# Orders of the small steps, a 17-pass down product and a written-out loop in a Mamba and FP4-FFN block

## The reference

```python
xz = x @ W_in                                    # 256 -> 2 x 512
x_conv = silu(conv1d(x_proj, 4 taps) + conv_b)   # causal, per channel
ssm = x_conv @ W_xproj                           # 33 columns: delta, B (16), C (16)
delta = softplus(ssm[..., 0])
h_mean = einsum('bld,bln->bdn', x_conv, delta * B) / L
y = (einsum('bdn,bln->bld', h_mean, C) + D * x_conv) * silu(z)
x = layernorm(x + y @ W_out)
h = silu(fp4(x) @ fp4(w_gate).T) * (fp4(x) @ fp4(w_up).T)     # 256 -> 704
out = layernorm(x + fp4(h) @ fp4(w_down).T)                   # 704 -> 256
```

## Time and profile before

| | us |
|---|---|
| median of 3 runs | 2334.24 (2331.59 to 2337.22) |
| the profiled execution | 2339.92 |
| its span, first to last instruction | 2338.1 |

### The profile page before, as it was taken

How to read it: one execution, slowest core, us unless ns; L and a number is a source line. 1 busy time by engine, 2 the same in 40 slices (tenths; PEclk the granted TensorE clock), 3 DMA queues, 4 the chain that set the end, 5 groups by cost and what they waited for, 6 DMA issues and landing times.

```text
span 2338.1 us, 38729 instructions
## 1 busy us (share of the span) xinstructions
PE 2050.8 (88%) x10532; PEld 1615.6 (69%) x10532; DVE 1701.5 (73%) x3292; ACT 1279.5 (55%) x2612; POOL 988.0 (42%) x1643
## 2 busy tenths in 40 slices
PE   2887799999899998999999999899989999888886
PEld 1555577777777777777777777777767777666665
DVE  6223477877787777777777787878778877777775
ACT  2556555655555656555655565555555655433343
POOL 2222344444444444444444444444444444434342
PEclk9879999999999999999999999999999999888898
DMA  2223322222222222222222222222222222111100
GB/s 74 86 72 113 111 93 95 84 86 83 94 85 83 92 96 86 78 88 95 84 92 85 95 84 86 82 87 92 93 83 83 97 84 86 52 57 55 57 30 14
DMA packets 132401, 191.35 MB, mean 82 GB/s; under 512 B 15024, under 2 KB 66096, under 8 KB 132144
## 3 DMA queue, kind: packets, MB, share of 16 engines
q1 hardware_dynamic: 132144, 188.42, 24.4%
HBM read 104.48 MB, written 83.89 MB: 81 GB/s over the span
## 4 chain that ended last, share of the span: by engine, by line
DVE 35%; PE 35%; issue 17%; ACT 10%; DVEq 1%; POOL 1%; SPq 0%; ACTq 0%; DMA 0%; POOLq 0%
PE pgu L483 9%; PE pd L483 7%; PE pc L557 5%; DVE acc L866 5%; DVE hbuf L802 4%; PE pb L483 4%; DVE g L946 4%; DVE hbuf L929 4%; PE pa L483 3%; ACT hbuf L717 2%; DVE hbuf L808 2%; DVE qsx L795 2%; PE pc L569 2%; DVE qsh L795 2%; DVE hqT L938 2%
## 5 line engine op out<-in xcount | busy, mean ns | idle before, releaser
L483 PE MATMUL pgu<-wgu_hi,xqT 128*128 128x512 f32 (+1 forms) x1536 | 437.8, 394 | 3.5 <-ACT xqT L762 1.7
L483 PE MATMUL pd<-wd_hi,hqT 128*128 128x256 f32 (+1 forms) x1536 | 344.9, 306 | 32.6 <-DVE r L959 28.2
L675 ACT ACTIVATE dev<-r,sum 128x256 f32<-128x256 f32 x256 | 130.1, 508 | 405.4 <-DVE r L959 253.9
L427 POOL TENSOR_TENSOR hq<-hnq,qsh 128x704 f32<-128x704 bf16 x128 | 177.7, 1388 | 378.9 <-DVE hnq L811 378.9
L483 PEld LDWEIGHTS pgu<-wgu_hi,xqT 128*128 128x128 f32 x1536 | 286.7, 194 | 68.5 <-issue 6.0
L483 PEld LDWEIGHTS pd<-wd_hi,hqT 128*128 128x128 f32 (+1 forms) x1536 | 267.3, 198 | 59.0 <-issue 38.8
L546 PE MATMUL pd<-wout,g 128*128 128x256 f32 x1024 | 254.8, 392 | 0.0
L483 PE MATMUL pgu<-wgu_lo,xqT 128*128 128x512 f32 (+1 forms) x768 | 233.8, 386 | 0.0
L483 PE MATMUL pd<-wd_lo,hqT 128*128 128x256 f32 (+1 forms) x768 | 224.7, 293 | 0.0
L414 POOL TENSOR_TENSOR acc<-acc,tap 128x512 f32<-128x512 f32 x128 | 163.0, 1274 | 133.9 <-ACT tap L740 133.9
L866 DVE SCALAR_TENSOR_TENSOR acc<-xps,cw,acc 128x512 f32<-128x512 f32 x256 | 195.0, 762 | 33.2 <-POOL acc L414 28.7
(11 more groups left out here) (132 smaller groups left out, 4545.0 us busy)
## 6 DMA issues: line engine op xcount, KB each, us to landing
sz_hbm<-szs SPq DMA_DIRECT2D x128, 256.0 KB, 2.1
xc_hbm<-xcs SPq DMA_DIRECT2D x128, 256.0 KB, 2.0
xl<-xc_hbm SPq DMA_DIRECT2D x128, 256.0 KB, 2.8
zl<-sz_hbm SPq DMA_DIRECT2D x128, 256.0 KB, 3.0
xin<-in_L_attn_x_dram SPq DMA_DIRECT2D x32, 512.0 KB, 4.4
xres<-in_L_attn_x_dram SPq DMA_DIRECT2D x128, 128.0 KB, 2.3
out_dram<-outb SPq DMA_DIRECT2D x128, 128.0 KB, 1.7
scratch<-in_L_attn_W_in_dram SPq DMA_DIRECT2D x1, 1024.0 KB, 7.2
```

The lines of the kernel that those rows point to most:

```text
L427: pool.tensor_tensor(blocks(hq[:, 0:FF]), blocks(hnq[:, :]), spread(qsh[:, 1, :]), ALU.mult).then_inc(hprod_done, 1)
L483: mm = pe.matmul(bank, lhsT, rhs, start=(m == 0), stop=(m == len(pairs) - 1))
L675: act.activation(dev[:, :], r, ACT.Square, bias=total[:, :], scale=-1.0 * DM, accum_out=ssq[:, :]).then_inc(ssq_done, 1)
```

## The change

- VectorE makes the skip product right after gate times up, ahead of h's absolute maximum and low parts. GpSimd multiplies g by silu(z) ahead of adding the first tap.
- ScalarE makes the gate's silu ahead of the conv's, and copies the transposed conv output and transposed x ahead of the squared deviations and the Abs of h.
- The three rows of scales become the innermost axis: an operand steps over three elements.
- `walk` has no loop; all 39 groups are written out.
- The down product's sixth chunk: h's last 64 columns are written twice (GpSimd, one more product), so that their transposes fill 128 rows; the weights hold the high part in rows 0 to 63 and the low part in rows 64 to 127. One pass of 128 rows makes high x high and high x low. At the start GpSimd copies the last 64 weight columns twice, and a zero fill is gone.

```diff
-        qsx = sb("qsx", [P, 3, QX])
+        qsx = sb("qsx", [P, QX, 3])
...
-        qsh = sb("qsh", [P, 3, QH])
+        qsh = sb("qsh", [P, QH, 3])
...
-        def walk(body, fori, last=0):
-
-            for g in range(2 * SPS):
-                body(g, g % SPS, g // SPS)
-            with fori(2, B - last) as b:
-                for s in range(SPS):
-                    body(b * SPS + s, s, b)
-            for g in range(NSUP - last * SPS, NSUP + LAG + 2):
+        def walk(body):
+
+            for g in range(NSUP + LAG + 2):
                 body(g, g % SPS, g // SPS)
...
+            pool.wait_ge(wq_ready, 3)
+            for h in range(KM):
+                rest = quant_w[2][:, h * FF + FC * P:(h + 1) * FF]
+                pool.tensor_copy(twice_d[:, h * P:h * P + FR], rest)
+                last = pool.tensor_copy(twice_d[:, h * P + FR:(h + 1) * P], rest)
+            last.then_inc(wq_ready, 1)
...
                         pool.tensor_copy(hist[:, j, :], xps[:, ST:ST + KC - 1])
-                        wait_apart(pool, (first_tap, u + 1))
-                        pool.tensor_tensor(acc[:, :], acc[:, :], tap0[:, :], ALU.add).then_inc(tap_done, 1)
                     if p2:
 
                         pool.wait_ge(yd_done, w + 1)
                         pool.wait_ge(zl_landed[j % 2], 16 * (2 * i + j // 2 + 1))
                         pool.tensor_tensor(g[:, second(s) % 2, j, :], g[:, second(s) % 2, j, :], zl[:, j % 2, :],
                                            ALU.mult).then_inc(g_ready, 1)
+                    if p1:
+                        wait_apart(pool, (first_tap, u + 1))
+                        pool.tensor_tensor(acc[:, :], acc[:, :], tap0[:, :], ALU.add).then_inc(tap_done, 1)
...
+                        pool.tensor_tensor(blocks(hq[:, FF:(FC + 1) * P]), blocks(hnq[:, FC * P:FF]),
+                                           spread(qsh[:, FC * P // QB:QH, 1]), ALU.mult)
                         pool.tensor_tensor(blocks(hq[:, 0:FF]), blocks(hnq[:, :]),
-                                           spread(qsh[:, 1, :]), ALU.mult).then_inc(hprod_done, 1)
+                                           spread(qsh[:, :, 1]), ALU.mult).then_inc(hprod_done, 1)
...
+                pairs += [(hqT[:, FC, :], wd_hi[:, FC, :]),
+                          (hqT[0:FR, 2 * FC + 1, :], wd_hi[0:FR, FC, :])]
                 split_product(pd[:, 0:DM], DM, pairs).then_inc(dn_pe, 1)
...
+                    if exists(tg):
+                        act.wait_ge(gu_pe, tg + 1)
+                        at_least(act, hq_link, 6 * tg)
+                        act.activation(hbuf[:, 0:FF], pgu[:, 0:FF], ACT.Silu).then_inc(sg_ready, 1)
                     if exists(v):
...
+                    if j != 1 and exists(v):
+                        act.wait_ge(xct_pe, v + 1)
+                        act.activation(xct[:, :, jb * P:(jb + 1) * P],
+                                       pa[:, :].rearrange("p (t n) -> p t n", t=TPS), ACT.Copy)\
+                            .then_inc(xct_copied, 1)
+                    if exists(tx):
+
+                        act.wait_ge(xq_pe, tx + 1)
+                        act.activation(xqT[:, 0:KM, :], pe_[:, 0:DM].rearrange("p (c n) -> p c n", c=KM), ACT.Copy)\
+                            .then_inc(xqT_hi, 1)
                     if exists(to):
                         deviations(r_done, to, r1[:, j, :], sum1, ssq1, ssq1_done)
...
                         dve.tensor_tensor(h, h_big, pgu[:, FF:2 * FF], ALU.mult).then_inc(h_done, 1)
+                    if p2:
+
+                        dve.wait_ge(y_pe, w + 1)
+                        dve.wait_ge(xl_landed[j % 2], 16 * (2 * i + j // 2 + 1))
+                        at_least(dve, o_pe, 4 * i - 4)
+                        dve.scalar_tensor_tensor(g[:, second(s) % 2, j, :], xl[:, j % 2, :], dsk[:, j:j + 1], pc[:, :],
+                                                 ALU.mult, ALU.add).then_inc(yd_done, 1)
+                    if exists(tg):
                         dve.wait_ge(h_done, tg + 1)
                         q_absmax(h, small_h).then_inc(hq_link, 1)
```

More of the change, by code:

```diff
@@ L354, in body @@
                         q.dma_start(sz_hbm[u], szs[:, j % 2, :]).then_inc(sz_saved[j % 2], 16)
-            walk(body, q.Fori, last=1)
+            walk(body)
             for k in range(2):
@@ L406, in body @@
                         at_least(pool, xq_pe, tx)
[L407 removed]
+                        pool.tensor_tensor(blocks(xv[:, :]), blocks(xnq[:, :]), spread(qsx[:, :, 1]),
                                            ALU.mult).then_inc(xprod_done, 1)
@@ L454, in weight_groups @@
                         groups.append((P, pieces, wgu_hi[:, k, lo:lo + width], wgu_lo[:, k, lo:lo + width]))
-            for c in range(FC + 1):
-                m = P if c < FC else FR
-                pieces = [(quant_w[2][:, h * FF + c * P:h * FF + c * P + m], P) for h in range(KM)]
-                groups.append((m, pieces, wd_hi[0:m, c, :], wd_lo[0:m, c, :]))
+            for c in range(FC):
+                pieces = [(quant_w[2][:, h * FF + c * P:h * FF + (c + 1) * P], P) for h in range(KM)]
+                groups.append((P, pieces, wd_hi[:, c, :], wd_lo[:, c, :]))
+            pieces = [(twice_d[:, h * P:(h + 1) * P], P) for h in range(KM)]
+            groups.append((P, pieces, wd_hi[:, FC, :], None))
             return groups
         W_GROUPS = weight_groups()
-        W_NEEDS = [1] * 4 + [2] * 4 + [3] * (FC + 1)
+        W_NEEDS = [1] * 4 + [2] * 4 + [3] * FC + [4]
         @block.tensor
@@ L610, in down_projection @@
                 pairs = []
-                for c in range(FC + 1):
-                    m_ = P if c < FC else FR
-                    pairs += [(hqT[0:m_, c, :], wd_hi[0:m_, c, :]),
-                              (hqT[0:m_, c, :], wd_lo[0:m_, c, :]),
-                              (hqT[0:m_, FC + 1 + c, :], wd_hi[0:m_, c, :])]
+                for c in range(FC):
+                    pairs += [(hqT[:, c, :], wd_hi[:, c, :]),
+                              (hqT[:, c, :], wd_lo[:, c, :]),
+                              (hqT[:, FC + 1 + c, :], wd_hi[:, c, :])]
+                pairs += [(hqT[:, FC, :], wd_hi[:, FC, :]),
+                          (hqT[0:FR, 2 * FC + 1, :], wd_hi[0:FR, FC, :])]
                 split_product(pd[:, 0:DM], DM, pairs).then_inc(dn_pe, 1)
@@ L747, in body @@
                                        scale=rs2[:, :]).then_inc(out_ready, 1)
-                    if exists(to):
-                        deviations(r_done, to, r1[:, j, :], sum1, ssq1, ssq1_done)
-                    if exists(tg):
-                        act.wait_ge(hq_link, 6 * tg + 4)
-                        act.activation(hbuf[:, 0:FF], hbuf[:, FF:2 * FF], ACT.Abs, scale=TWO22)\
-                            .then_inc(hbig_ready, 1)
                     if j != 1 and exists(v):
@@ L763, in body @@
                             .then_inc(xqT_hi, 1)
+                    if exists(to):
+                        deviations(r_done, to, r1[:, j, :], sum1, ssq1, ssq1_done)
+                    if exists(tg):
+                        act.wait_ge(hq_link, 6 * tg + 4)
+                        act.activation(hbuf[:, 0:FF], hbuf[:, FF:2 * FF], ACT.Abs, scale=TWO22)\
+                            .then_inc(hbig_ready, 1)
                     if p1:
@@ L843, in _ @@
                 dve.wait_ge(wt_hi, n + 1)
+                if lo is None:
+                    dve.tensor_tensor(hi[FR:P, :], (pa, pb)[n % 2][FR:P, 0:DM], hi[FR:P, :], ALU.subtract)\
+                        .then_inc(wt_lo, 1)
+                    continue
                 dve.tensor_tensor(lo, (pa, pb)[n % 2][0:rows, 0:lo.shape[1]], hi, ALU.subtract)\
                     .then_inc(wt_lo, 1)
-            small_x = [qsx[:, r, :] for r in range(3)]
-            small_h = [qsh[:, r, :] for r in range(3)]
+            small_x = [qsx[:, :, r] for r in range(3)]
+            small_h = [qsh[:, :, r] for r in range(3)]
             def body(g_, s, b):
@@ L940, in body @@
                                           hqT[:, 4:6, :], ALU.subtract).then_inc(hqT_lo, 1)
-                    if p2:
-                        dve.wait_ge(y_pe, w + 1)
-                        dve.wait_ge(xl_landed[j % 2], 16 * (2 * i + j // 2 + 1))
-                        at_least(dve, o_pe, 4 * i - 4)
-                        dve.scalar_tensor_tensor(g[:, second(s) % 2, j, :], xl[:, j % 2, :], dsk[:, j:j + 1], pc[:, :],
-                                                 ALU.mult, ALU.add).then_inc(yd_done, 1)
                     if exists(tg):
```

21 lines of the change are left out of this document (9 added, 12 removed).

## The result

The changed kernel took 2115.76 us (median of 4 runs, 2111.68 to 2122.11) beside 2335.73 us before (2331.59 to 2339.78): a ratio of 0.9061, 95% interval 0.9030 to 0.9091. The forecast was 2135 us, 2087 to 2241. The profiled execution took 2118.45 us with a span of 2116.7, against 2338.1 before: 221.4 us less.

The account below looks back on a forecast made before the run. TensorE plus its stalls was taken to bound the pipeline, VectorE's chain the drain. Savings 125 + 4 + 12 + 23 + 35 = 199 us from the profiled 2339.9 gave 2141, or 2135 us as a median; range 2087 to 2241.

Parts of the forecast that it names:

- Waits of 105.8 us gone: Full pipeline: TensorE's waits on the skip product and the transposed conv's copy vanish, saving 125 us.
- Skip product and copies, one sum: Full pipeline: moving VectorE's skip product and ScalarE's copies up removes waits of 67.4, 21.6 and 16.8 us, summed to 105.8.
- Room for the low parts and for r: Pipeline step: VectorE's low parts (by 1366.93, wanted after 1367.1) and residual sum come before TensorE asks, so no new wait.
- stall-moves rival: Pipeline: the stall only moves to the x transposes or down projection; only loop and pass gain, 2289 us; chance 0.06.
- Group with the state sum: Pipeline: one group in four, with a finished sequence's state sum on VectorE, stays some 3 us longer than plain groups.
- The pass, 12 us: Down product: 17 passes save 0.12 us a step, 0.48 a group, 12 us in 25 groups.
- The loop, 23 us: Pipeline: writing out all groups removes five jumps back at 4.7 us each, 23 us; bounds 13 and 39.
- starving of straight code: Looped groups written out: TensorE would stand for instructions, costing 226 us against the gain, 2361 us; chance 0.02.
- Scales, zero: VectorE's scale operation: interleaving the scales gains nothing; bounds were nothing or 0.5 us twice a step.
- The rival in which the scale's wait goes: Drain: interleaving lifts the scale's wait for GpSimd, drain 20 to 40 us shorter, pipeline unchanged, 2105 us; chance 0.12.
- The drain, 35 us: After the full pipeline: 0.75 us a step over some 25 steps, 19 us, plus 15 for the clock; 10 to 75.
- VectorE takes over: Pipeline: VectorE's chain with its own waits holds groups at 62.5 us and the drain gives little, 2241 us; chance 0.17.

Follow-up runs that it names:

- e1_loop: The changed kernel with the loop over sequences put back: 2137.47 us, ratio 0.9156 to the kernel before.
- e3_accum: The changed kernel with the scale operation in its accumulator form, the floor of the scale left out: 2118.27 us, ratio 0.9062 to the kernel before.
- e2_rows: The changed kernel with the scales in three rows again, as before: 2113.58 us, ratio 0.9051 to the kernel before.

## Why the prediction was right, and where its steps were off

**Waits of 105.8 us gone, 125 us with overlap and two more groups**: right in kind, a little short. A plain group lost 5.74 us; less the 0.46 that the pass measured, 5.28, or 132 us in 25 groups. The forecast's sum took 10 of at most 18 us for the overlap that a stall also costs, 5.0 a group; its plain group of 59.9, which came out at 59.2, took none, 4.6. Measured is nearly the whole: (105.8 + 18) / 23 = 5.4. The rows agree: the state projection now starts 0.16 us before the shown end of what precedes it, and its eight take 0.98 us for 1.08.

**Skip product and copies, one sum**: right as a sum, but the text treated them as two savings of 89 and 16.8 us. Alone they bring 57 and 59, together 166. A stall removed alone only reaches the next late operation.

**Room for the low parts and for r**: held. No such wait of TensorE in the pipeline; the stall-moves rival is out for the change, though with the skip product alone the stall does move, to the transposes of C.

**Group with the state sum, "some 3 us more in one of four", kept**: wrong, the largest miss in the pipeline. It is 59.57 against 59.21, 0.4 us. The step that failed took the extra for work that stays. Before, the group with the state sum (the first line) and the plain one behind it read:

```profile
438.27:506.12 67.85, 62.32 (x329) 49.61 (x329) 53.20 (x103) 39.52 (x81) 30.10 (x52) 0.97 0.26 86
506.12:571.08 64.96, 60.74 (x330) 48.30 (x329) 51.57 (x101) 39.06 (x81) 30.61 (x52) 1.00 0.27 89
```

Of the 2.9 us more, 1.3 are TensorE idle (5.5 us for 4.2; its waits before the state projection are 4.1 for 2.6) and 1.6 are matmuls that take longer, at a clock of 0.97 for 1.00: a VectorE that was already late made TensorE wait longer, and with it the clock was lower. In the loop these groups had 2.9 to 4.5 us over a plain one, 22.0 in all six; the change's six have 2.3. The reorders alone left 2.4 us in the first of them; the new silu order and the 17th pass take 1.0 each, and with the accumulator's scales or the later maxima the group is as the others. Of the 183.9 us that groups 7 to 31 lost, 132 are stalls, 11.5 passes, 18.8 jumps (e1_loop) and 19.7 this; 2 are left.

**The pass, 12 us**: its own 0.12 us held (59.67 against 59.21). The whole was 32 by the ratio: besides 11 in plain passes, 6 us through the state sum's group and 14 in a drain at a lower clock, most of which is not shown to be the pass's.

**The loop, 23 us**: 22 by the ratio. 18.8 of it in the pipeline, 3.8 a jump rather than 4.7. The working that gave 4.7 took 3.2 us for each of five groups with a state sum, where they had 3.8 in the mean; with that it would have been (39.4 - 19.1) / 5 = 4.1. No starving of straight code: plain groups are within 0.03 us of each other.

**Scales, zero**: held, for the reason given beside it. The rival in which the scale's wait goes, priced at 20 to 40 us of the drain, would have given nothing: with the wait gone in e3_accum the time is the same.

**Hq product in two pieces**: 0.30 + 1.42 us, starting 0.25 apart, against 1.38: 0.3 us for 0.25, hidden.

**The drain, 35 us**: 37.2 came, partly by luck. The xq wait went and the divide of h fell from 1.27 to 0.89 as priced; a plain step fell by 0.86 where 0.75 was forecast, and the steps that were 14.84 us became 12.8 at most. But the drain of equal code differs by 9 us from one execution to another. With both reorders alone the stretch from group 31 on fell from 428.7 to 406.4 us; of the other 20.7 down to 385.7, which came with a clock of 0.96 for 0.91, the pass itself is 3 and the rest is not assigned. The 15 us for the clock were a choice with no row behind them but their upper bound.

**VectorE takes over**: not in the pipeline, where 51.6 of 59.0 us were no bound (nor at 57.3); in the drain it does.

Sum of the misses against the profiled execution, 2141 to 2118.5: 7 us of stalls, 20 of the state sum's groups, 2 of the drain and 2 unassigned more than forecast; 4 of the jumps, 4 of the filling (0.3 us came) and 0.5 of the passes less: 22 us. The forecast lay 19 us above the measured median, so the sum missed by a tenth of the gain, with the largest term right in kind and one term left out.

## What to carry to other kernels

Here a list of waits priced removing all of them, not one: the next late operation stood behind each, and two reorders brought three times what either did. An extra that appears in one group of four can be a lateness, not work; ask what it becomes when its engine is ahead. Where two engines wait for each other in turn, a cut in one ring alone may buy nothing, as with the accumulator's scales in the old order; look for both before choosing an edit. Before a few us at the start or the end of a profile are explained, see how much equal code differs there.

## What the runs showed of the hardware that was not expected

- A scale operation on 128 x 16 fp32 values took 0.18 us at the least and 1.0 in the median beside a busy GpSimd, whether its operands step by one element or three (e2_rows, after); in the form with an accumulator it took 0.18 each time, plus a read of 0.08 (e3_accum).
- Dodging one meeting with GpSimd can make another: with the scale free the x divide went from 0.42 to 0.47 us in the median, and with h's maxima later as well to 0.67.
- Equal code from group 31 on took 385.7 and 394.4 us, at clocks of 0.96 and 0.93; with h's maxima later the clock there was 0.98, with full steps of 11.95 us each.
- A lateness cost more than its wait: the group with the state sum stood 1.3 us longer, and its matmuls took 1.6 us longer at a mean clock of 0.97 (before).
- Jumps back to the start of the loop's long body cost 18.8 us of the pipeline, 3.8 for each of five (e1_loop).
